# A cross attention in 64 by 64 TensorE tiles, its mask on TensorE, its values copied by VectorE

## What is computed

```python
q, k, v = heads(ln(x) @ W_q.T), heads(ctx @ W_k.T), heads(ctx @ W_v.T)   # 16 heads of 16
scores = einsum(q, k) / sqrt(16)                                         # 8 x 16 x 64 x 1601
p = softmax(where(mask, scores, -1e10), axis=-1)
x = x + einsum(p, v) @ W_proj.T + b_proj
```

## Time and profile before

| | us |
|---|---|
| median of 3 runs | 2487.47 (2486.67 to 2489.14) |
| the profiled execution | 2501.07 |
| its span in the profile | 2499.3 |
| this layer in the span | about 322 to 732 |
| PE / DVE / ACT / POOL busy over the span | 2236.3 / 1650.0 / 1243.2 / 808.3 |

### The profile page before, as it was taken

The page is one execution under the profiler, slowest core; times in us unless marked ns, Lnnn a source line. Parts: engine busy times, 40 slices in busy tenths (PEclk is TensorE's granted clock), DMA queues, the critical chain, the costliest instruction groups (busy, mean ns, idle before and its releaser), DMA issues. The chain is left out here.

```text
span 2499.3 us, 50978 instructions
## 1 busy us (share of the span) xinstructions
PE 2236.3 (89%) x20593; PEld 1417.7 (57%) x20650; DVE 1650.0 (66%) x3182; ACT 1243.2 (50%) x2071; POOL 808.3 (32%) x660
## 2 busy tenths in 40 slices
PE   6885779999978889999999999699879999998898
PEld 4764445666654555656655666356546555566554
DVE  4987456555548756888888854644576666665577
ACT  2326234555554225555555554566436555563565
POOL 5610052233206112321233300045445455433254
PEclk8998899999989989999999999899999999999999
DMA  3200453423313047676776764133322323220231
GB/s 113 71 7 1 144 136 103 107 78 106 79 66 106 13 118 144 121 133 133 151 146 122 125 113 80 34 102 102 116 67 67 86 69 86 69 67 23 71 96 60
DMA packets 358618, 226.84 MB, mean 91 GB/s; under 512 B 289913, under 2 KB 326610, under 8 KB 358386
## 3 DMA queue, kind: packets, MB, share of 16 engines
q1 hardware_dynamic: 355314, 215.20, 35.5%
q0 software_dynamic: 3072, 8.39, 1.2%
HBM read 114.87 MB, written 0.52 MB: 46 GB/s over the span
## 5 line engine op out<-in xcount | busy, mean ns | idle before, releaser
L3950 POOL TENSOR_TENSOR l2x_rows<-l2x_rows,l2x_one 128x256 f16<-128x256 f32 (+1 forms) x91 | 89.2, 1006 | 379.6 <-DVE l2x_rows L1507 354.5
L100 PE MATMUL PS<-hot 128*128 128x512 f16 x460 | 134.3, 427 | 82.1 <-DVE l0a_g L1119 17.5
L4054 PE MATMUL PS<-l2x_rows,l2x_pth 128*128 128x512 f16 x832 | 200.3, 379 | 1.7 <-DVE l2x_mean L4263 1.7
L3711 DVE CUSTOM_DVE_ANT_0 l1x_junk<-PS,l1x_bias 128x1024 bf16<-128x1024 f32 (+1 forms) x128 | 123.2, 991 | 73.6 <-PE PS L3371 72.7
L4256 DVE TENSOR_TENSOR l2x_pl<-l2x_sc,l2x_ph 128x1664 f16<-128x1664 f32 x64 | 125.1, 1954 | 44.6 <-ACT l2x_ph L4133 43.9
L4151 ACT ACTIVATE l2x_meanT<-PS 128x256 f32<-128x256 f32 x64 | 24.5, 383 | 250.5 <-PE PS L4016 250.5
L4241 DVE CUSTOM_DVE_ANT_0 l2x_sc<-PS,l2x_bias 128x1665 f32<-128x1665 f32 x64 | 120.9, 1889 | 36.3 <-issue 35.0
L3711 DVE CUSTOM_DVE_ANT_0 l3x_junk<-PS,l3x_bias 128x1024 bf16<-128x1024 f32 (+1 forms) x128 | 123.6, 991 | 24.3 <-PE PS L3371 21.6
L4008 PE MATMUL PS<-l2x_kh,l2x_qth 128*128 128x512 f16 (+1 forms) x512 | 131.9, 339 | 1.5 <-issue 1.5
L4008 PE MATMUL PS<-l2x_kh,l2x_qtl 128*128 128x512 f16 (+1 forms) x512 | 131.9, 339 | 0.0
L4008 PE MATMUL PS<-l2x_kl,l2x_qth 128*128 128x512 f16 (+1 forms) x512 | 131.9, 339 | 0.0
(11 more groups left out here) (866 smaller groups left out, 6109.0 us busy)
## 6 DMA issues: line engine op xcount, KB each, us to landing
l2f_unit<-in_L_ffn_units_dram SPq DMA_DIRECT2D x36, 384.0 KB, 3.1
l3f_unit<-in_L_ffn_units_dram SPq DMA_DIRECT2D x34, 384.0 KB, 3.0
l1x_kst<-l1x_kh SPq DMA_DIRECT2D x128, 100.1 KB, 2.2
l3x_kst<-l3x_kh SPq DMA_DIRECT2D x128, 100.1 KB, 2.2
l2x_rows<-in_ctx_dram SPq DMA_DIRECT2D x8, 1536.0 KB
l1x_ctx<-in_ctx_t_dram SPq DMA_DIRECT2D x7, 1601.0 KB, 7.3
l3x_ctx<-in_ctx_t_dram SPq DMA_DIRECT2D x7, 1601.0 KB, 7.0
l1x_kst<-l1x_kl SPq DMA_DIRECT2D x64, 100.1 KB, 2.2
```

Source lines behind the costliest of these rows:

```text
L100: self.nc.tensor.matmul(self.PS[:, bank, :], self.hot[:, 0:P], self.hot[:], start=True, stop=True)
L3711: v.tensor_tensor_reduce(junk[:, slot(it), 0:n], slot_banks(it)[:, 0:n], bias[:, 0 if normed else b % 2, at:at + n], 1.0, LOWEST, ALU.add, ...
L3950: last = nc.gpsimd.tensor_tensor(high[:, at], of[:, at], one[0:p, at].unsqueeze(2).unsqueeze(3).to_broadcast([p, i, NC, P]), ALU.mult)
L4054: nc.tensor.matmul(PS[:, ACC, :], pth[:, u % 2, m, :], rows2[:, b % 2, :, :, m, :], start=(m == 0), stop=False)
```

## The change

Only layer_1_xattn calls the new function, `row_tiled_attention`; the later layer stays as it was.

- The contraction is laid out anew. Feature f of a pair takes four neighbouring rows: constant, high, low, high. One head's 16 features fill 64 rows, so the heads of a pair are the two halves (r) of the 128 rows, without zeros. Every score matmul is 64 rows by 64 columns of the array.
- Turned scores: one `turned(b, m)` fills both banks at once: four mask matmuls of 512 columns and 8 pairs x 2 halves of the keys x 2 heads = 32 matmuls of 64 columns. It waits for both exponentials of the block before. DVE adds no mask any more; `mask_columns` and `bias_t` go.
- A items: still sixteen a batch, now two pairs and 401 keys (398 the last), four matmuls, and two DVE reductions each instead of one. They stand first in the steps that have another item.
- V is copied out by DVE, in the order of its items.
- Queries are split and turned as f16 instead of fp32, with one full copy instead of two masked ones. M has two transposes and two row copies instead of four and one.
- The constant rows, now every fourth, come by two transfers of 32 partitions x 8 x 1601 f16, after the first loads. The exponentials and items of ACT are ordered per key block instead of per step. WARM is 3 matmuls after every A item instead of 3 and 2.

```diff
-    ON_VECTOR = list(range(4))
+    ON_VECTOR = list(range(4)) if normed else []
...
-        steps = [[("K", 0, 0)], [], [("K", 0, 1), R_], [("K", 1, 0)], [E], [("K", 1, 1)], [("V", 0, 0)], [O_], [A[0]], [A[1]],
-                 [("V", 1, 0), A[2]], [A[3]], [P_, A[4]], [("V", 2, 0), A[5]], [A[6]], [A[7]], [("V", 3, 0), A[8]], [A[9]],
-                 [("M", 0, 0), A[10]], [A[11]], [A[12]], [A[13]], [A[14]], [A[15]], [], [("M", 1, 0)]]
+        steps = [[("K", 0, 0)], [], [("K", 0, 1), R_], [("K", 1, 0)], [E], [("K", 1, 1)], [("V", 0, 0)], [O_], [A[0]], [A[1]],
+                 [A[2], ("V", 1, 0)], [A[3]], [P_, A[4]], [A[5], ("V", 2, 0)], [A[6]], [A[7]], [A[8], ("V", 3, 0)], [A[9]],
+                 [A[10], ("M", 0, 0)], [A[11]], [A[12]], [A[13]], [A[14]], [A[15]], [("M", 1, 0)], []]
...
+                        for x, part in ((1, kh), (2, kl), (3, kh)):
+                            sp.dma_start(kst[x::PARTS, b % 2, c * RC + j, :],
+                                         part[j * F:(j + 1) * F, c, :]).then_inc(stacked[c * RC + j], 16)
...
+                        at, n = chunks[j]
+                        for i in range(2):
+                            for r in range(2):
+                                rows = slice(r * S, (r + 1) * S)
+                                last = nc.tensor.matmul(PS[i * S:(i + 1) * S, bank + r, 0:n], qst[rows, b, 2 * c + i, :],
+                                                        kst[rows, b % 2, 2 * c + i, at:at + n], start=True, stop=True)
...
+                def turned(b, m):
...
+                            pe.wait_ge(exp_done, e)
+                    if m == 0:
+                        pe.wait_ge(row_made, G2 * (b + 1))
...
+                                    nc.tensor.matmul(PS[at:at + w_, S_BANK + r, :], of_bias[:, m * P + at:m * P + at + w_], one_hot[half, :],
+                                                     start=(x == 0), stop=False, skip_group_check=True)
+                    for u in range(R):
+                        for at, w_ in keys:
+                            for r in range(2):
+                                rows = slice(r * S, (r + 1) * S)
+                                last = nc.tensor.matmul(PS[at:at + w_, S_BANK + r, u * S:(u + 1) * S],
+                                                        kst[rows, b % 2, u, m * P + at:m * P + at + w_], qst[rows, b, u, :],
+                                                        start=not on_tensor, stop=not on_tensor or u == R - 1, skip_group_check=True)
...
+                    elif kind == "V":
+                        dve.wait_ge(made, number[it] + 1)
...
+                        v.tensor_scalar(
+                            v33[0:part, b % 2, VT * c:VT * c + m, :, 0:DH],
+                            slot_banks(it)[0:part, 0:m * D].rearrange("p (m h f) -> p m h f", m=m, h=H), 1.0 / SW, None,
+                            ALU.mult).then_inc(v_read, 1)
...
+                        for r in range(2):
+                            last = v.tensor_tensor_reduce(junk[:, slot(it), r * BANK:r * BANK + n], PS[:, 2 * slot(it) + r, 0:n],
+                                                          bias[:, 0 if normed else b % 2, at:at + n], 1.0, LOWEST, ALU.add, ALU.max,
+                                                          rmax[:, r, c, j:j + 1])
...
-    context_attention(k, "l1x", normed=False, finished=("l0x", "l0a", "l0f"))
+    row_tiled_attention(k, "l1x", normed=False, finished=("l0x", "l0a", "l0f"))
```

More of the change, by code:

```diff
@@ L4369, in heads, with heads_by_half @@
         return w.reshape(2, 2, 4, D // H, D).transpose(1, 0, 2, 3, 4).reshape(2, P, D)
+    def heads_by_half(w):
+        return w.reshape(2, 4, 2, D // H, D).transpose(0, 2, 1, 3, 4).reshape(2, P, D)
     def columns(v):
@@ L4415, in laid_out @@
         a[f"L1_xattn_{name}_t"] = a.pop(f"L1_xattn_{name}").T
-    a["L1_xattn_W_proj_t_heads"] = heads(a.pop("L1_xattn_W_proj").T)
+    a["L1_xattn_W_proj_t_heads"] = heads_by_half(a.pop("L1_xattn_W_proj").T)
     both = a.pop("L2_xattn_Wkv")
@@ L4423, in laid_out @@
     a["fside_columns"] = tiled(a["fside_SxS2_0"])
-    a["mask_columns"] = tiled(a["mask_Bx1xSxS2_bk0"][:, 0])
     n = np.arange(D)
```

684 lines of the change are left out of this document (added).

## The result

The changed kernel takes 2509.8 us (median of 4 runs, 2507.6 to 2514.1) where the kernel before takes 2488.3 in the same measurement: a ratio of 1.0088, with a 95% interval of 1.0075 to 1.0101. That is 21.5 us slower. Forecast were 3.7 us faster and a range that ended at 2499.

What follows compares the result with a forecast made beforehand. PE looked bound, but GpSimd's context split fixed 12.5 us per batch, so only the rest could shrink. Preparation -2.2, six batches -3.6, last preparation -1.2, bare batch +3.3: -3.7 us, median 2483.8, range 2473 to 2499.

Steps and rivals of the forecast that it cites:

- A key block T: Mask and turned scores of one key block on PE: 0.50 us, with both ends kept, up to 0.96.
- Quartets at 0.032: In the turned scores, four 64-column matmuls in four array quadrants run together, costing 0.032 us per quartet.
- Rival 1: Turned scores: weight loads sharing a row half take turns, 0.057 us per quartet; in all +5.9 us, 2493.4; chance 0.22.
- rival 2: Turned scores: four quadrants take two turns, 0.063 us per quartet; about +30 us, 2517; chance 0.09.
- rivals 3 and 4: 3: projection slots free sooner, total falls 7 to 13, 2477, chance 0.17; 4: context split holds nothing, 2446, chance 0.04.
- Maximum items of 0.99 on DVE: Each 401-column maximum item, with its two reductions, takes DVE 0.99 us between the value projections.
- K11's wait of about 1.0 us: PE idles about 1.0 us before the last key projection, waiting for the bank slot of the one before it.
- The bare batch at 1.84: Last batch: key blocks wait for both exponentials, 1.84 us each instead of 1.57; 3.3 us more.
- K00 still released by the context split: Next batch's first key projection still waits for GpSimd's context split, with 1.5 to 2 us of PE idle time before.
- Walk from K00 to V3: From a batch's first key projection to its last value projection: 0.6 us less in each of six batches, 3.6 together.
- Preparation: Before the batches: f16 queries start the first maximum at 364.3 instead of 367.58; first key projection 2.2 us earlier.
- The last part: After the final value projection: 10.4 us for 11.6 to batch 8's first scores, then 3.3 more in the bare batch.

Runs made afterwards that it cites:

- the first run: Changed kernel with only the 65-key last block reordered ("edge mended"): everything of its 64 keys, then of the last key; 1.0008 of the kernel before.

## Why the prediction was wrong

**The step that failed** is "A key block T is 0.03 + 0.22 + 8 x 0.032 = 0.50 us". It was right for 12 of the 13 key blocks (0.49) and taken for all 13. The prediction had the price that the last one needed: "I take 0.095 us for each change of tile shape", from rows 2. It did not ask what tiles the code makes of 65 keys. Some 17 changes at 0.095 are 1.6 us; less the 0.5 of idle time before K00 that is 1.1 in six batches, and twice 1.6 behind the last V3: 9.8 more, a sum of +6.1 us instead of -3.7. At the measured 2.3 it is 6 x 1.8 + 2 x 2.3 = 15.4, and +11.7. The loops stood in the diff. A second number had to fail with it. The 0.5 us of idle time is the measured one; the prediction expected 1.5 to 2 before K00, and that much would have hidden most of the edge in the six batches, at either price. The first run shows 0.54; where the rest went is said below. The rest of the error is the half clock that followed (2.3, 0.5 and 0.3 us at the three K00s, and 1.5 at the end) and the terms below.

**Part by part.** Quartets at 0.032: right (0.031). Rival 1, two turns of the loads, and rival 2 are out by that; of the gains of rivals 3 and 4 nothing came. (The terms that rival 1 lists give 5.3 to 6.5 us, depending on whether the 1.2 of the last preparation counts, and not just the 5.9 of its sum.) Maximum items of 0.99 on DVE: right, two reductions start 0.495 apart. K11's wait of about 1.0 us: right (0.96 at 528.46, 0.97 in the first run). The bare batch at 1.84: right (1.86), 12 x 0.30 = 3.6 us for 3.3. "K00 still released by the context split": wrong in the changed kernel, right once the edge is mended; PE's idle time had gone to waits for DVE's maximum items, the exponentials and K11 instead.

**Walk from K00 to V3**, 0.6 a batch: with the edge mended it is 0.2 to 0.4 in the five batches with E, and the first batch, which I had left unchanged, is 0.4 longer. Five batches and the first together gave 1.0 us for 3.0. The mechanism was right and the size a third. Up to V0 the walk is right (16.0 us for 15.9). From V0's end it gave V1, V2 and V3 3.6, 9.8 and 15.95 us, and in the first run they start after 3.75, 9.97 and 16.27 in a batch without P, PE waiting for DVE's maximum items each time; in the kernel before it is 3.59, 9.98 and 16.38. So the error lies between V0 and V3, where DVE's queue sets the pace.

**Preparation**, 2.2 us: nothing came. The first maximum starts 37.5 us after the stage's start, exactly as before, where I had it 3.3 earlier. DVE's rows say why:

```profile
342.44 1.32 DVE L4386 TENSOR_SCALAR l1x_v<-l1x_xn 128x1024 f16<-128x1024 f32 x1
343.80 1.32 DVE L4387 COPY l1x_v<-l1x_v 128x1024 f16<-128x1024 f16 x1
344.93 2.46 DVE L4388 SCALAR_TENSOR_TENSOR l1x_v<-l1x_xn,l1x_v 128x1024 f16<-128x1024 f32 x1
347.19 2.50 DVE L4477 TENSOR_SCALAR l1x_v<-PS 128x1024 f32<-128x1024 f32 x2
```

Writing the f16 parts interleaved takes 5.0 us where the three fp32 steps took 3.2 (353.22 to 356.38 before), the last of them 2.46 for 1.22. I had costed turning and copying the queries, and not making them. Behind them the two values copies stand in the queue. That these two took the whole 2.2 us is argued from the rows; the run with ACT's copies shows 0.6 of it.

**The last part**: the 10.4 us that I gave from V3's end to the first scores of batch 8 were 11.5 in the first run, as good as no gain on the 11.6 before; then 3.6 for 3.3; and 1 to 2 us of stops for instructions, a cost that the prediction did not have at all. In the changed kernel the edge comes twice on top, 4.6 us for the 1.5 that it still costs in the first run, with 1.5 of half clock at the very end.

**Outside the stage** the code is the same, and from its end to the end of the program the traces give 1760.1 us before, 1764.8 after and 1755.8 to 1763.4 in the other runs. That spread carries nothing of the change that I can show.

The rivals had the sign on the wrong ground: 0.31 of the chance stood on slower by slow quartets, none on the last block. The range ended 11 us short of the result.

## What to carry to other kernels

When a tile is made smaller, walk the loop for the remainder too: a matmul of one column costs little by itself and 0.13 us each time it stands between wider ones, so keep equal shapes together or pad. Count PE's instructions per microsecond as well as its columns; a layout that nearly halves the columns of a block (0.9 to 0.5 us) and takes 136 instructions for 84 can be bound by their supply. And where two limits give the same period, taking away one shows nothing: take away each and then both.

## What the runs showed of the hardware

- A step from a 64-column to a 1-column tile takes 0.145 us and back 0.12 in the new layout, 0.17 and 0.15 in the old one with 128 columns streamed; two halves of 64 columns by turns cost nothing. 18 us in a kernel of 2490 came from cutting eight matmuls per batch.
- Four 64 by 64 quadrants of the array work at once: 32 matmuls of 64 columns in 0.25 us, 8 ns apart on average.
- PE stops each 256 instructions where it would take them faster than about 256 per 3.5 us: 0.15 to 1.2 us in the bare batch, up to 1.8 idle elsewhere. At 254 in 3.6 us (104 per key block of 1.49) no stop over 0.25 us was left. Moving the 1.6 MB load moved the long stops into it; why only some of the loads have one was not settled.
- Three of the seven sparse blocks of 2.8 us in the loop were followed by 3.4 to 6.8 us at 1.2 GHz, the longest with PE fully busy in 5 us of it, at a cost of 2.3 us. Without such a block the clock fell in four other runs, twice of these behind a stop of 1.6 to 1.8 us.
